# Turning tile rows with VectorE and SBUF-to-SBUF transfers in place of TensorE transposes

## Chip, cores and metric

One core of one Trainium2 chip. The metric is the device time of one execution in microseconds. The kernel before took 358.4 us (median of three runs, 358.2 to 358.91).

## What is computed

The input `x` has 64 batches of 32 rows with 256 features. Every batch goes through one attention layer and two MLPs, and then through three adapter layers whose weights are picked by the batch's role (one of three):

```python
attn = softmax((x @ Wq) @ (x @ Wk).T * scale)
attn_out = (attn @ (x @ Wv)) @ Wp + bp
cms_out = gelu(attn_out @ cW1 + cb1) @ cW2 + cb2 + one_hot(code)
x1 = clip(x + cms_out + gelu(concat(attn_out, cms_out) @ mW1 + mb1) @ mW2 + mb2, 0, 1)
for layer in range(3):            # x1 is the first hidden_states
    h = gelu(hidden @ W_down[role] + b_down[role]) @ W_up[role] + b_up[role]
    hidden = layernorm(hidden + h) * gamma[role] + beta[role]
```

## The kernel before

The 2048 rows are sorted by role and cut into 16 tiles of 128 rows, four batches each. A tile is "pure" if its four batches have one role. Tiles 4 and 5 (`MIXED`) take what is left over: their four batches have four sets of weights, so each of their layers loads four weight blocks of 256.5 KB where a pure tile loads one.

The MLPs run over groups of rows: three groups of 512 rows and two of 256 (`GROUPS`). Their steps are written in a list: "H n" computes the hidden block n on TensorE, "D n" brings it down into the results, and between them ScalarE makes the gelu and a high part (`h_hi`) and VectorE the low part (`h_lo`). TensorE is fed by one matmul after another this way.

The three adapter layers of the tiles lie between these steps. While group 1 runs, tiles 0 to 3 go through their layers (wave 1); while group 2 runs, tiles 4 to 7 (wave 2); then tiles 8 to 11 and 12 during the two small groups, and the last three at the end. A wave has 14 spots, one behind an H step each, and in a wave each tile starts one spot behind the one before. For a tile and layer, the down product is at one spot, the up product one spot on, the norm two spots on, and the next layer's down product four spots on. "(4, 1)" below is tile 4, layer 1, with layers counted from 0.

The down product needs the tile with features on the partitions, while the norm leaves rows there. So for layers 1 and 2 `half` on TensorE turns the normed rows `window_x` by two 128x128 transposes into a PSUM bank (L1512), and ScalarE copies it to `window_xT` (L841), which the down product reads (L1481; L1478 for mixed tiles). Layer 0 reads `xT`, which is there already.

SyncE's queue carries nearly all loads. It works through the items (tile, layer) in the order of their down products, weights of an item first (`window_weights`), then the rows (gamma, beta, and for layer 0 an up bias) of the item before (`window_rows`). Mixed tiles' layer 1 weights lie in a region that the attention uses until it is done (`at_done`). For each mixed tile at layer 0 it reads four roles from a table (L572) and then waits for `at_done`:

```python
roles_of[w] = ([role(MIXED[0] + WIN * MIXED.index(w) + q) for q in range(WIN)] if w in MIXED ...
if w in MIXED:
    if layer == 0:
        sp.wait_ge(at_done, VB * NG)
```

TensorE's down product of a mixed tile waits for all four of its blocks.

Of the kernel before, what the change touches and what calls it, by code (L numbers as in the profile page):

```python
# [12 lines left out]
P = 128  # L13
# [29 lines left out]

ROLE_COLS = NW - len(MIXED) + MIXED_BATCHES
# [12 lines left out]
def build(nc, x, codes, roles, Wq, Wk, Wv, Wp, bp, cW1, cb1, cW2, cb2, mW1, mb1, mW2, mb2, adapters, out):  # L57
# [3 lines left out]
    with ExitStack() as ctx:  # L61
# [107 lines left out]
        window_xT = sb("window_xT", [P, 2, VB, P])  # L169
        window_h = sb("window_h", [P, 2, P])  # L170

# [84 lines left out]
        earlier_ready = sem("earlier_ready")  # L256
        role_row_ready = sem("role_row_ready")
        roles_turned = sem("roles_turned")
        own_ready = sem("own_ready")
        roles_counted = sem("roles_counted")  # L260
# [6 lines left out]
        code_ready = sem("code_ready")  # L267
# [55 lines left out]
        emptied = {b: sem(f"emptied{b}") for b in (2, 3, 5, 6, 7)}  # L323
        first_w_in = sem("first_w_in")
# [89 lines left out]
        def turned(wave, spot):  # L414
            return [(w, at // 4 + 1) for w, at in turns(wave, spot) if at % 4 == 3 and 1 <= at // 4 + 1 < LAYERS]
# [94 lines left out]
        def _(sp):  # L510
# [76 lines left out]
            def window_weights(w, layer):  # L587
                slot, k = slot_of(w), item(w, layer)
                if layer == 0:
                    roles_of[w] = ([role(MIXED[0] + WIN * MIXED.index(w) + q) for q in range(WIN)] if w in MIXED  # L590
                                   else [role(role_col(w))])
# [12 lines left out]

# [307 lines left out]
        def _(dve):  # L912
# [3 lines left out]
            dve.tensor_scalar(earlier[:, :], batch_id[:, :], own_id[0:B, 0:1], None, ALU.is_gt).then_inc(earlier_ready, 1)  # L916
# [19 lines left out]
            dve.tensor_tensor(own_onehot[:, :], role_id[:, :], own, ALU.is_equal).then_inc(own_ready, 1)  # L936
# [4 lines left out]
            dve.wait_ge(own_ready, 1)  # L941
            dve.wait_ge(roles_counted, 1)
# [18 lines left out]
            dve.tensor_scalar(code_rep[:, :], ones[:, :], code_col[:, :], None, ALU.mult).then_inc(code_ready, 1)  # L961
# [31 lines left out]
            def attention_part(stage_name, g):  # L993
# [18 lines left out]
                if stage_name == "P":  # L1012
# [6 lines left out]
                    dve.wait_ge(pd_clear, 2)  # L1019
# [653 lines left out]
```

## Time and profile before

| | |
|---|---|
| median of three runs | 358.4 us |
| profiled execution, its own time | 357.08 us |
| its span | 355.2 us |
| PE (TensorE) busy | 344.4 us, 97% |
| DVE (VectorE) busy | 202.6 us, 57% |
| ACT (ScalarE) busy | 169.2 us, 48% |
| DMA moved | 46.14 MB, mean 130 GB/s |

The span runs from the first instruction to the end of the last. "Busy" is the union of an engine's instructions; a matmul's duration in the records is longer than the distance to the next one's start, since they are pipelined.

### The profile page before, as it was taken

How to read it: one execution, taken by the hardware profiler on the slowest of the kernel's cores; microseconds unless marked ns; L12 is line 12 of the kernel's file. 1: busy time of each engine (PE TensorE's matmuls, PEld its weight loads, DVE VectorE, ACT ScalarE, POOL GpSimd, SP SyncE). 2: the span in 40 equal slices, each digit the busy share in tenths (PEclk: the TensorE clock that was granted, in tenths of full speed). 3: DMA queues.
4: the chain of work that ended last, by engine and by line, in shares of the span. 5: the costliest groups of instructions: out<-in, count | busy, mean ns of one | idle time of the engine just before them, and what ended most of it. 6: DMA issues, size and time to landing. Idle time of an engine off the chain costs nothing.

```text
span 355.2 us, 6665 instructions
## 1 busy us (share of the span) xinstructions
PE 344.4 (97%) x2252; PEld 287.1 (81%) x2252; DVE 202.6 (57%) x488; ACT 169.2 (48%) x338; POOL 62.0 (17%) x94
## 2 busy tenths in 40 slices
PE   7799999999999999999999999999999999999994
PEld 6587678787878888888886777877899999999962
DVE  5066375433353875466545666554589777554584
ACT  3555685453642563463336454443455544543421
POOL 2700230000040110012311111003322024100231
PEclk9999998999999999999999999999999999999998
DMA  6674899284020141310075898412856533188001
GB/s 211 199 221 146 206 126 144 57 192 109 2 54 6 60 119 62 101 49 6 25 253 163 226 257 306 104 31 74 227 145 188 168 104 108 59 273 345 23 2 45
DMA packets 30646, 46.14 MB, mean 130 GB/s; under 512 B 4779, under 2 KB 15348, under 8 KB 30612
## 3 DMA queue, kind: packets, MB, share of 16 engines
q1 hardware_dynamic: 28852, 41.72, 43.0%
q0 software_dynamic: 1392, 3.80, 3.9%
q8 instruction: 18, 0.29, 0.4%
q10 hardware_dynamic: 368, 0.20, 0.2%
q14 instruction: 16, 0.13, 0.1%
HBM read 43.60 MB, written 4.48 MB: 135 GB/s over the span
## 4 chain that ended last, share of the span: by engine, by line
PE 91%; ACT 3%; DVE 2%; issue 2%; POOL 1%; POOLq 0%; DVEq 0%
PE bank L332 12%; PE bank L334 12%; PE bank L333 12%; PE bank L1437 9%; PE bank L1442 8%; PE bank L1438 8%; PE bank L1481 4%; PE bank L1460 4%; PE bank L1343 2%; PE bank L1361 2%; PE bank L1512 2%; PE bank L1301 2%; PE bank L1242 1%; PE bank L1560 1%; PE bank L1457 1%
## 5 line engine op out<-in xcount | busy, mean ns | idle before, releaser
L798 ACT ACTIVATE h_full<-bank,bias 128x512 f32<-128x512 f32 (+1 forms) x80 | 48.2, 603 | 108.3 <-PE bank L334 98.0
L1035 DVE TENSOR_TENSOR h_lo<-h_full,h_hi 128x512 fp32r<-128x512 f32 (+1 forms) x80 | 46.8, 585 | 63.2 <-ACT h_hi L802 60.8
L718 POOL TENSOR_TENSOR rstd<-moments,minus_half 128x1 f32<-128x1 f32 x39 | 24.3, 623 | 168.1 <-DVE moments L1101 167.9
L802 ACT ACTIVATE h_hi<-h_full 128x512 fp32r<-128x512 f32 (+1 forms) x80 | 43.7, 547 | 2.5
L1093 DVE TENSOR_TENSOR window_y<-bank,window_x 128x256 f32<-128x256 f32 x39 | 16.5, 423 | 38.3 <-PE bank L1460 28.9
L1437 PE MATMUL bank<-h_hi,c_hi 128*128 128x512 f32 (+1 forms) x80 | 30.8, 393 | 0.2
L1437 PE MATMUL bank<-h_hi,m_hi 128*128 128x512 f32 (+1 forms) x80 | 30.2, 387 | 0.2
L332 PE MATMUL bank<-at_hi,c_hi 128*128 128x512 f32 (+1 forms) x80 | 29.3, 366 | 0.0
L332 PE MATMUL bank<-at_hi,m_hi 128*128 128x512 f32 (+1 forms) x80 | 29.2, 364 | 0.0
L334 PE MATMUL bank<-at_lo,c_hi 128*128 128x512 f32 (+1 forms) x80 | 27.9, 348 | 0.0
L334 PE MATMUL bank<-at_lo,m_hi 128*128 128x512 f32 (+1 forms) x80 | 27.8, 348 | 0.0
L333 PE MATMUL bank<-at_hi,m_lo 128*128 128x512 f32 (+1 forms) x80 | 27.8, 347 | 0.0
L333 PE MATMUL bank<-at_hi,c_lo 128*128 128x512 f32 (+1 forms) x80 | 27.8, 347 | 0.0
L1438 PE MATMUL bank<-h_hi,c_lo 128*128 128x512 f32 (+1 forms) x80 | 27.6, 354 | 0.0
L690 POOL DMA_INDIRECT xr<-in_x,row_idx x16 | 16.4, 1025 | 62.5 <-PE bank L1343 52.9
L1438 PE MATMUL bank<-h_hi,m_lo 128*128 128x512 f32 (+1 forms) x80 | 27.2, 349 | 0.0
L332 PE MATMUL bank<-cms_hi,m_hi 128*128 128x512 f32 (+1 forms) x70 | 24.3, 346 | 0.0
L333 PE MATMUL bank<-cms_hi,m_lo 128*128 128x512 f32 (+1 forms) x70 | 24.3, 346 | 0.0
L334 PE MATMUL bank<-cms_lo,m_hi 128*128 128x512 f32 (+1 forms) x70 | 24.3, 346 | 0.0
L1442 PE MATMUL bank<-h_lo,c_hi 128*128 128x512 f32 (+1 forms) x80 | 22.4, 362 | 0.1
L1084 DVE SCALAR_TENSOR_TENSOR window_x<-window_y,rstd,adapter_rows 128x256 f32<-128x256 f32 x39 | 18.7, 480 | 4.9 <-POOL rstd L718 3.2
L1442 PE MATMUL bank<-h_lo,m_hi 128*128 128x512 f32 (+1 forms) x80 | 21.4, 348 | 0.0
(239 smaller groups left out, 733.9 us busy)
## 6 DMA issues: line engine op xcount, KB each, us to landing
adapter_w<-packed_w SPq DMA_DIRECT2D x44, 256.5 KB, 3.5
adapter_rows<-packed_rows SPq DMA_DIRECT2D x36, 256.0 KB, 5.2
stage<-in_L_cond_mW SPq DMA_DIRECT2D x6, 512.0 KB, 6.3
mixed_w<-packed_w SPq DMA_DIRECT2D x8, 256.5 KB, 5.0
stage<-in_L_cond_cW SPq DMA_DIRECT2D x4, 512.0 KB, 4.7
last_w<-packed_w SPq DMA_DIRECT2D x2, 769.5 KB, 6.4
up_bias<-in_L_cond_b_up SPq DMA_DIRECT2D x12, 128.0 KB, 6.1
adapter_rows<-packed_rows SPq DMA_DIRECT2D x24, 64.0 KB
```

The source lines that it names most:

```text
L332: pe.matmul(o, w_hi_ap, r_hi_ap, start=first, stop=False)
L333: pe.matmul(o, w_lo_ap, r_hi_ap, start=False, stop=False)
L334: return pe.matmul(o, w_hi_ap, r_lo_ap, start=False, stop=last)
L718: pool.tensor_tensor(slot.rstd[:, :], slot.moments[:, 1:2], minus_half[:, :], ALU.pow)\
L798: act.activation(h_full[:, n % 2, rows], bank[n % 2][:, rows], ACT.Gelu, bias=bias[:, b:b + 1])\
L802: act.activation(h_hi[:, n % 2, rows], h_full[:, n % 2, rows], ACT.Copy).then_inc(h_hi_ready, 1)
L1035: dve.tensor_tensor(h_lo[:, n % 2, rows], h_full[:, n % 2, rows], h_hi[:, n % 2, rows].bitcast(F32), ALU.subtract).then_inc(h_lo_ready, 1)
L1084: dve.scalar_tensor_tensor(slot.x[:, :], slot.y[:, :], slot.rstd[:, :], slot.rows[:, 1, :], ALU.mult, ALU.add).then_inc(slot.x_ready, 1)
L1093: dve.tensor_tensor(slot.y[:, :], bank[6][:, 0:V], slot.x[:, :], ALU.add).then_inc(emptied[6], 1)
L1437: pe.matmul(results[ob][:, rows], high(cols), h_hi[:, n % 2, rows], start=(j == 0), stop=False)
L1438: pe.matmul(results[ob][:, rows], low(cols), h_hi[:, n % 2, rows], start=False, stop=False)
L1442: ins = pe.matmul(results[ob][:, rows], high(cols), h_lo[:, n % 2, rows], start=False, stop=(j == HB - 1))
```

## The change

For tiles 0 to 7 (`SPREAD`), the 16 turns for layers 1 and 2 leave TensorE and ScalarE. VectorE turns `window_x` in 32x32 blocks into a new tile `block_rows`, and SyncE's queue then moves the blocks by four transfers, one for each quarter of 32 rows, into `window_xT`, of which there are now three instead of two. A transfer carries 128 pieces of 256 bytes. The down product waits for the transfers' semaphore. SyncE waits for VectorE before each move, and for the down product three moves back.

The loads of the mixed tiles change their place. After `at_done`, `mixed_weights_ahead` reads the roles and loads all four layer 1 blocks and two of the four layer 0 blocks, for tile 4 and then for tile 5. The other two blocks of layer 0 follow for each tile. The rows of item (3, 2) go ahead of the wait for `at_done` instead of behind the first mixed weights. Four semaphores of the setup are merged into others, with the same waits.

```diff
+SPREAD = WAVES[1] + WAVES[2]
+RING = 3
...
-        window_xT = sb("window_xT", [P, 2, VB, P])
+        window_xT = sb("window_xT", [P, RING, VB, P])
         window_h = sb("window_h", [P, 2, P])
+        block_rows = sb("block_rows", [P, 2, V])
...
-            return [(w, at // 4 + 1) for w, at in turns(wave, spot) if at % 4 == 3 and 1 <= at // 4 + 1 < LAYERS]
+            return [(w, at // 4 + 1) for w, at in turns(wave, spot)
+                    if at % 4 == 3 and 1 <= at // 4 + 1 < LAYERS and w not in SPREAD]
+
+        def spread(wave, spot):
+            return [(w, layer + 1) for w, layer in norms(wave, spot) if layer + 1 < LAYERS and w in SPREAD]
+
+        moves = {}
+        for wave in WAVES:
+            for spot in range(SPOTS):
+                for move in spread(wave, spot):
+                    moves[move] = len(moves)
+
+        def moved(n):
+            return next(move for move, m in moves.items() if m == n)
+
+        def blocks_of(n):
+            return window_xT[:, n % RING, :, :].rearrange("p k m -> p (k m)").rearrange("p (q k r) -> p q k r", q=Q, k=VB)
+
+        def move_is_in(engine, n):
+            engine.wait_ge(blocks_in[n % RING], 16 * Q * (n // RING + 1))
...
+                if layer == 0 and w not in MIXED:
+                    roles_of[w] = [role(role_col(w))]
                 if w in MIXED:
                     if layer == 0:
-                        sp.wait_ge(at_done, VB * NG)
                         sp.wait_ge(slot.x_ready, k)
                     elif layer == 2:
                         sp.wait_ge(filled[6], use["U", w, 0] + 1)
-                    for q in range(WIN):
+                    for q in ((0, 1), (), range(WIN))[layer]:
                         load_w(batch_w(w, layer, q), roles_of[w][q], layer, mixed_in[MIXED.index(w)][layer % 2])
                 else:
                     if k >= 2:
                         sp.wait_ge(slot.x_ready, k if w - SLOTS in MIXED and layer == 0 else k - 1)
                     load_w(slot.w[:, k % 2, :], roles_of[w][0], layer, slot.w_in[k % 2])
+
+            def mixed_weights_ahead():
+                sp.wait_ge(at_done, VB * NG)
+                for n, w in enumerate(MIXED):
+                    roles_of[w] = [role(MIXED[0] + WIN * n + q) for q in range(WIN)]
+                    for q in range(WIN):
+                        load_w(batch_w(w, 1, q), roles_of[w][q], 1, mixed_in[n][1])
+                    for q in range(2, WIN):
+                        load_w(batch_w(w, 0, q), roles_of[w][q], 0, mixed_in[n][0])
+
+            def move_blocks(w, layer):
+
+                n = moves[w, layer]
+                sp.wait_ge(blocks_turned, n + 1)
+                if n >= RING:
+                    sp.wait_ge(filled[7], use["D", *moved(n - RING)] + 1)
+                for q in range(Q):
+                    sp.dma_start(blocks_of(n)[:, q, :, :].rearrange("p k r -> p (k r)"),
+                                 block_rows[quarter(q), n % 2, :].rearrange("p (f m) -> p f m", f=Q))                        .then_inc(blocks_in[n % RING], 16)
...
             for n, w, layer in items:
+                if n and items[n - 1][1:] in moves:
+                    move_blocks(*items[n - 1][1:])
+                if (w, layer) == (MIXED[0], 0):
+                    window_rows(*items[n - 1][1:])
+                    mixed_weights_ahead()
                 window_weights(w, layer)
-                if 0 < n <= len(items) - len(ending):
+                if 0 < n <= len(items) - len(ending) and (w, layer) != (MIXED[0], 0):
                     window_rows(*items[n - 1][1:])
...
+                for w, layer in spread(wave, spot):
+                    n = moves[w, layer]
+                    dve.wait_ge(slot_of(w).x_ready, item(w, layer - 1) + 1)
+                    if n >= 2:
+                        move_is_in(dve, n - 2)
+                    dve.transpose(block_rows[:, n % 2, :].rearrange("p (f k r) -> p k f r", f=Q, k=VB),
+                                  slot_of(w).x[:, :].rearrange("p (k i f) -> p k f i", f=Q, k=VB)).then_inc(blocks_turned, 1)
...
+                    elif w in SPREAD:
+                        move_is_in(pe, moves[w, layer])
...
-                        rows = (xT[:, vb, columns(w)] if layer == 0
-                                else window_xT[:, order["T", w, layer] % 2, vb, :])
+                        rows = (xT[:, vb, columns(w)].rearrange("p (q r) -> p q r", q=Q) if layer == 0
+                                else blocks_of(moves[w, layer])[:, :, vb, :] if w in SPREAD
+                                else window_xT[:, order["T", w, layer] % 2, vb, :].rearrange("p (q r) -> p q r", q=Q))
```

On TensorE, at the first removed pair (`xT` is the layer 0 start of tile 1; `window_x0` is tile 0's rows). Before:

```order
L1442 MATMUL bank2<-h_lo,c_hi 128x512 [waits h_lo_ready]
L1442 MATMUL bank3<-h_lo,c_hi 128x512
L1504 MATMUL bank6<-ident,xT 128x128 [waits emptied6]
L1504 MATMUL bank6<-ident,xT 128x128
L1512 MATMUL bank7<-ident,window_x0 128x128 [waits emptied7,window_x_ready0]
L1512 MATMUL bank7<-ident,window_x0 128x128
L332 MATMUL bank0<-at_hi,c_hi 128x512 [waits gelu_done]
L333 MATMUL bank0<-at_hi,c_lo 128x512
```

The same place on TensorE now:

```order
L1491 MATMUL bank2<-h_lo,c_hi 128x512 [waits h_lo_ready]
L1491 MATMUL bank3<-h_lo,c_hi 128x512
L1556 MATMUL bank6<-ident,xT 128x128 [waits emptied6]
L1556 MATMUL bank6<-ident,xT 128x128
L333 MATMUL bank0<-at_hi,c_hi 128x512 [waits gelu_done]
L334 MATMUL bank0<-at_hi,c_lo 128x512
```

The two transposes of `window_x0` are gone; nothing took their place.

On VectorE, where tile 0's rows come out of the norm (`window_x0`), before:

```order
L1084 SCALAR_TENSOR_TENSOR window_x0<-window_y0,rstd0,adapter_rows0 128x256 [waits norm_step0,rstd_ready0]
L1093 TENSOR_TENSOR window_y1<-bank6,window_x1 128x256 [waits emptied6,filled6]
L1035 TENSOR_TENSOR h_lo<-h_full,h_hi 128x512 [waits h_hi_ready]
L1099 BN_STATS stats1<-window_y1 128x6 [waits emptied6]
L1101 BN_AGGR moments1<-stats1 128x2 [waits norm_step1]
```

The same place on VectorE now:

```order
L1126 SCALAR_TENSOR_TENSOR window_x0<-window_y0,rstd0,adapter_rows0 128x256 [waits norm_step0,rstd_ready0]
L1135 TENSOR_TENSOR window_y1<-bank6,window_x1 128x256 [waits emptied6,filled6]
L1141 STREAM_TRANSPOSE block_rows<-window_x0 128x2x4x32 [waits window_x_ready0]
L1077 TENSOR_TENSOR h_lo<-h_full,h_hi 128x512 [waits h_hi_ready]
L1148 BN_STATS stats1<-window_y1 128x6 [waits emptied6]
L1150 BN_AGGR moments1<-stats1 128x2 [waits norm_step1]
```

The block transpose stands ahead of the next `h_lo`. From the third move on it also waits for the move two back (`blocks_in`).

On SyncE's queue, where it waits for the attention's end (`adapter_w0` and `mixed_w4` are the four layer 0 blocks of tile 4; the roles were read ahead of this wait), before:

```order
L575 ISA [waits window_x_ready0,at_done]
L575 DMA adapter_w0<-packed_w 128x513
L575 ISA
L575 DMA adapter_w0<-packed_w 128x513
L575 ISA
L575 DMA mixed_w4<-packed_w 128x513
L575 ISA
L575 DMA mixed_w4<-packed_w 128x513
L579 ISA [waits window_x_ready3]
L579 DMA adapter_rows3<-packed_rows 128x512
L572 TENSOR_LOAD role_table
```

The same wait on SyncE's queue now (`second_w` is a layer 1 block):

```order
L592 TENSOR_LOAD role_table [waits at_done]
L592 ISA x2
L592 TENSOR_LOAD role_table
L592 ISA x2
L592 TENSOR_LOAD role_table
L592 ISA x2
L592 TENSOR_LOAD role_table
L592 ISA x2
L595 ISA
L595 DMA second_w<-packed_w 128x513
L595 ISA
L595 DMA second_w<-packed_w 128x513
```

Behind it stand two more layer 1 blocks of tile 4, two of its layer 0 blocks, four role reads and six blocks for tile 5. Only then, on the same queue, comes the rest of layer 0:

```order
L595 DMA mixed_w5<-packed_w 128x513
L595 ISA
L595 DMA mixed_w5<-packed_w 128x513
L595 ISA [waits window_x_ready0]
L595 DMA adapter_w0<-packed_w 128x513
L595 ISA
L595 DMA adapter_w0<-packed_w 128x513
L595 ISA [waits window_x_ready1]
L595 DMA adapter_w1<-packed_w 128x513
L595 ISA
L595 DMA adapter_w1<-packed_w 128x513
```

The last block of (4, 0) was the fourth load behind the wait, with its roles read already; it is now the fourteenth, with eight role reads between.

## Rows read from the trace of the kernel before

**Rows 1.** The page: span, and busy time by engine.

```profile
span 355.2 us, 6665 instructions
...
PE 344.4 (97%) x2252; PEld 287.1 (81%) x2252; DVE 202.6 (57%) x488; ACT 169.2 (48%) x338; POOL 62.0 (17%) x94
```

**Rows 2.** The page: the chain that ended last, by engine.

```profile
PE 91%; ACT 3%; DVE 2%; issue 2%; POOL 1%; POOLq 0%; DVEq 0%
```

**Rows 3.** Line L1512, 110 to 255 us: duration min/median/max, first and last start.

```profile
L1512 PE MATMUL bank<-ident,window_x x32: 270/272/273, 126.7 to 246.0; 128*128 128x128 f32 x32
```

**Rows 4.** Timeline of PE (start, us): with a pair, and without.

```profile
130.12 0.63 PE L1442 MATMUL bank<-h_lo,c_hi 128*128 128x512 f32 x2
130.58 0.38 PE L1512 MATMUL bank<-ident,window_x 128*128 128x128 f32 x2
...
131.03 0.39 PE L333 MATMUL bank<-at_hi,c_lo 128*128 128x512 f32 x1
...
138.41 0.62 PE L1442 MATMUL bank<-h_lo,c_hi 128*128 128x512 f32 x2
...
139.10 0.39 PE L333 MATMUL bank<-at_hi,m_lo 128*128 128x512 f32 x1
```

**Rows 5.** Timeline of PE at the first D step of the second MLP: with, without.

```profile
145.01 0.39 PE L334 MATMUL bank<-cms_lo,m_hi 128*128 128x512 f32 x1
...
145.81 0.40 PE L1438 MATMUL bank<-h_hi,m_lo 128*128 128x512 f32 x1
...
68.44 0.39 PE L334 MATMUL bank<-cms_lo,m_hi 128*128 128x512 f32 x1
...
69.25 0.40 PE L1438 MATMUL bank<-h_hi,m_lo 128*128 128x512 f32 x1
```

**Rows 6.** Groups of VectorE by form: busy us, mean ns, idle before.

```profile
L1035 DVE TENSOR_TENSOR h_lo<-h_full,h_hi 128x512 fp32r<-128x512 f32 x48 | 33.2, 692 | 51.6 <-ACT h_hi L802 50.2 <-issue 1.3
...
L1093 DVE TENSOR_TENSOR window_y<-bank,window_x 128x256 f32<-128x256 f32 x39 | 16.5, 423 | 38.3 <-PE bank L1460 28.9 <-PE bank L1457 8.1 <-issue 1.3
...
L1021 DVE STREAM_TRANSPOSE pd<-expd 32x128 f32<-32x128 f32 x16 | 4.8, 303 | 0.3
```

**Rows 7.** Timeline: norm and next down product, tiles 0 and 4, layer 0 to 1.

```profile
120.28 0.47 DVE L1084 SCALAR_TENSOR_TENSOR window_x<-window_y,rstd,adapter_rows 128x256 f32<-128x256 f32 x1
...
128.75 0.61 PE L1481 MATMUL bank<-window_xT,adapter_w 128*128 128x128 f32 x4
...
198.16 0.48 DVE L1084 SCALAR_TENSOR_TENSOR window_x<-window_y,rstd,adapter_rows 128x256 f32<-128x256 f32 x1
...
207.44 0.65 PE L1478 MATMUL bank<-second_w,window_xT 128*32 128x128 f32 x16
```

**Rows 8.** SyncE's longest wait, 155 to 195 us, and its timeline behind it.

```profile
SPq L575 <- PE bank L334: 11.2, 1, 11.2
...
177.53 0.87 SPq L575 DMA_DIRECT2D adapter_w<-packed_w  x2
...
179.64 0.33 SPq L579 DMA_DIRECT2D adapter_rows<-packed_rows  x1
182.50 0.86 SPq L575 DMA_DIRECT2D adapter_w<-packed_w  x2
```

**Rows 9.** Weight loads 177 to 186 us, and small stores: issue to landing.

```profile
DMA to landing us min/median/max: 2.7/3.4/4.5
...
out<-last_x SPq DMA_DIRECT2D x4, 32.0 KB, 1.6
```

**Rows 10.** Stretch 179 to 183 us: busy by engine, PEclk, DMA share, GB/s.

```profile
179.00:183.00 4.00, 4.00 (x19) 3.29 (x18) 0.54 (x2) 1.47 (x3) 0.65 (x1) 1.00 0.92 329
```

**Rows 11.** Timeline of PE: the down product of (4, 0) starts.

```profile
190.52 0.30 PE L1478 MATMUL bank<-adapter_w,xT 128*32 128x128 f32 x2
```

**Rows 12.** The one stretch at the low clock, and the matmuls ahead of it.

```profile
59.80:63.20 3.40, 3.40 (x10) 2.62 (x9) 0.25 (x3) 0.00 (x0) 0.00 (x0) 0.50 0.63 73
...
L1373 PE MATMUL bank<-acol,prep_w x24: 165/250/250, 56.2 to 58.6; 128*128 128x1 f32 x24
```

More of the change, by code:

```diff
@@ L255, in build @@
         id_consts = sem("id_consts")
-        earlier_ready = sem("earlier_ready")
         role_row_ready = sem("role_row_ready")
         roles_turned = sem("roles_turned")
-        own_ready = sem("own_ready")
-        roles_counted = sem("roles_counted")
         more_consts = sem("more_consts")
@@ L266, in build @@
         onehot_ready = sem("onehot_ready")
-        code_ready = sem("code_ready")
         rows_turned = sem("rows_turned")
@@ L323, in build @@
         emptied = {b: sem(f"emptied{b}") for b in (2, 3, 5, 6, 7)}
+        blocks_turned = sem("blocks_turned")
+        blocks_in = [sem(f"blocks_in{n}") for n in range(RING)]
         first_w_in = sem("first_w_in")
@@ L588, in window_weights @@
                 slot, k = slot_of(w), item(w, layer)
-                if layer == 0:
-                    roles_of[w] = ([role(MIXED[0] + WIN * MIXED.index(w) + q) for q in range(WIN)] if w in MIXED
-                                   else [role(role_col(w))])
+                if layer == 0 and w not in MIXED:
+                    roles_of[w] = [role(role_col(w))]
                 if w in MIXED:
                     if layer == 0:
-                        sp.wait_ge(at_done, VB * NG)
                         sp.wait_ge(slot.x_ready, k)
@@ L915, in _ @@
             dve.wait_ge(id_consts, 3)
-            dve.tensor_scalar(earlier[:, :], batch_id[:, :], own_id[0:B, 0:1], None, ALU.is_gt).then_inc(earlier_ready, 1)
+            dve.tensor_scalar(earlier[:, :], batch_id[:, :], own_id[0:B, 0:1], None, ALU.is_gt).then_inc(pd_clear, 1)
             for a in (first_attention, second_attention):
@@ L935, in _ @@
             own = own_role.to_broadcast([B, ROLES])
-            dve.tensor_tensor(own_onehot[:, :], role_id[:, :], own, ALU.is_equal).then_inc(own_ready, 1)
+            dve.tensor_tensor(own_onehot[:, :], role_id[:, :], own, ALU.is_equal).then_inc(role_row_ready, 1)
             dve.tensor_tensor(upto, role_id[:, :], own, ALU.is_le)
@@ L940, in _ @@
             link(dve.tensor_copy(own_role_col[:, :], own_role))
-            dve.wait_ge(own_ready, 1)
-            dve.wait_ge(roles_counted, 1)
+            dve.wait_ge(role_row_ready, 2)
+            dve.wait_ge(roles_turned, 2)
             link(dve.tensor_copy(counts_i[:, :], totals))
@@ L960, in _ @@
             dve.wait_ge(more_consts, 2)
-            dve.tensor_scalar(code_rep[:, :], ones[:, :], code_col[:, :], None, ALU.mult).then_inc(code_ready, 1)
+            dve.tensor_scalar(code_rep[:, :], ones[:, :], code_col[:, :], None, ALU.mult).then_inc(onehot_ready, 1)
             dve.wait_ge(rows_turned, 1)
@@ L1018, in attention_part @@
                                            a.row_sum[:, 1, :].unsqueeze(2).to_broadcast([P, GT, T]), ALU.mult))
-                    dve.wait_ge(pd_clear, 2)
+                    dve.wait_ge(pd_clear, 3)
                     for q in range(Q):
@@ L1255, in _ @@
             pe.matmul(bank[4][0:B, 0:1], role_row[:, 1, :], ones[0:1, 0:1], start=True, stop=True).then_inc(roles_turned, 1)
-            pe.wait_ge(earlier_ready, 1)
-            pe.wait_ge(own_ready, 1)
+            pe.wait_ge(pd_clear, 1)
+            pe.wait_ge(role_row_ready, 2)
             pe.matmul(bank[5][0:B, 0:ROLES], ones[:, 0:B], own_onehot[:, :], start=True, stop=True)
             pe.matmul(bank[5][0:B, ROLES:2 * ROLES], earlier[:, :], own_onehot[:, :], start=True, stop=True)\
-                .then_inc(roles_counted, 1)
+                .then_inc(roles_turned, 1)
             turn_weights(0)
@@ L1271, in _ @@
             fold_weights(0, wT[:, 0], wT[:, 1])
-            pe.wait_ge(code_ready, 1)
+            pe.wait_ge(onehot_ready, 2)
             pe.matmul(bank[6][:, 0:B], code_rep[:, :], onehot[:, :], start=True, stop=True)
@@ L1477, in after @@
                             for q in range(WIN):
-                                ins = pe.matmul(bank[b][quarter(q), 0:KD], rows[:, quarter(q)], batch_w(w, layer, q)[:, down],
+                                ins = pe.matmul(bank[b][quarter(q), 0:KD], rows[:, q, :], batch_w(w, layer, q)[:, down],
                                                 start=(vb == 0), stop=(vb == VB - 1))
```

## Prediction, made before the changed kernel ran

> **What bounds the kernel now.** I read the page's busy times first: TensorE is busy for 344.4 of 355.2 us, and no other engine passes 57% [rows 1]. The chain of work that ended last lies on TensorE for 91% [rows 2]. Since a matmul's recorded end is modelled, a busy share doesn't prove that nothing waits, so I then read the timeline of PE for the distances from start to start. Between 110 and 255 us, where the two waves of the change lie, a 512-column matmul follows the last one every 0.23 us (0.69 for three [rows 4]), and the few longer steps are changes of form. So in this stretch TensorE's own instruction stream is the time. What leaves it is gained one to one, and what makes TensorE wait is lost one to one, since I see no later idle time that could give it back.
>
> The second thing to read is the load queue. SyncE sat 11.2 us in its longest wait of the stretch, until the attention's last product (bank, L334), and issued the first mixed weights right behind it, at 177.53 [rows 8]. TensorE wants them at 190.52 [rows 11]. This distance of 13 us is what the moved loads must fit into.
>
> **The change part by part.**
>
> *The transposes go.* 32 of them run between 126.7 and 246.0 us [rows 3], that is 16 pairs. Their recorded 272 ns is not what they cost. With a pair, the start of the two L1442 matmuls and that of L333 lie 131.03 - 130.12 = 0.91 us apart; at a like place without one, 139.10 - 138.41 = 0.69 [rows 4]. A pair costs 0.22 us. Two of the 16 cost nothing: where the second MLP's first D step waits for its `h_hi`, L334 to L1438 takes 145.81 - 145.01 = 0.80 with the pair and 69.25 - 68.44 = 0.81 without [rows 5]. The pair only filled a wait there, and this holds for tiles 3 and 7 at layer 1. So 14 x 0.22 = 3.1 us are gained. The Trainium skill, on the page "TensorE: Matmul & The Clock Gate", section "Part 4: PE-mode transpose", gives about 275 ns for one transpose in a kernel's context. The trace's 272 ns agrees as a duration; taken as a cost it would make the gain 32 x 0.275 = 8.8 us. The distances in the timeline decide for 3.1.
>
> *ScalarE loses 16 copies.* It is no bound, and nobody waits for it in this stretch but for `h_hi` at the two places above. Worth nothing; never a loss.
>
> *VectorE gets 16 block transposes.* The trace has none of 128x256. A block transpose of half the width takes 303 ns, an addition of the full width 423 ns [rows 6]. I take 0.42 us and allow 0.3 to 0.8. It stands ahead of the next `h_lo`, and the 48 large `h_lo` had 51.6 us of idle time before them, over 1 us each in the mean [rows 6]. Where there is less, TensorE still reads an `h_lo` only one D and one H step on, twelve matmuls of 0.23 us or more. So it costs nothing; without that cover, it would be 16 x 0.4 = 6.4 us.
>
> *The moves.* SyncE issues four transfers of 32 KB, one every 0.53 us (two span 0.87 and one 0.33 [rows 8]): 2.1 us. Nearest to their landing are the 32 KB stores at the end, 1.6 us, and the weight loads under traffic, 2.7 to 4.5 us [rows 9]. From the end of the norm to the data this is 0.4 (another addition on VectorE) + 0.4 + 2.1 + 1.6 to 4.5 = 4.5 to 7.4 us. The shortest distance of the 16 is that of (0, 1): 128.75 - 120.75 = 8.0 us [rows 7]; next is (4, 1) with 207.44 - 198.64 = 8.8 [rows 7], and the others reach to 18. So they are hidden. Queued behind SyncE's wait for a move are the weights and rows of the next items, whose products come later still.
>
> *The mixed loads.* Here I count every instruction of the queue. Before, TensorE's product (4, 0) needed the first four loads behind the wait. The last of them was issued at 179.1 (0.53 ahead of the rows' 179.64 [rows 8]) and landed at 183.6 (4.5, the maximum of [rows 9]), 7 us early. Now the order is: four role reads, six loads, four role reads, six loads, then the two that complete (4, 0). From the end of one issue to the next with four role reads between takes 182.50 - 179.97 = 2.5 us instead of 0.2 [rows 8], so the reads add 2.3. The first load is issued at 177.5 + 2.3 = 179.8, the sixth at 179.8 + 5 x 0.53 = 182.5, the seventh at 182.5 + 0.3 + 2.5 = 185.3, and the fourteenth at 185.3 + 7 x 0.53 = 189.0. Unhindered it lands at 189.0 + 2.7 = 191.7, after the 190.5 at which TensorE stands before it. But eight loads issued at 0.53 us run into each other: at the measured 329 GB/s [rows 10] one of 262.7 KB takes 0.80 us. The first of the eight lands at 185.3 + 2.7 = 188.0, the last at 188.0 + 7 x 0.80 = 193.6. In the burst of before, the fourth load landed at 183.6, which is 0.9 later than this reckoning gives (180.2 + 3 x 0.80 = 182.6); at that burst's own pace, (183.6 - 180.2) / 3 = 1.12, the last of eight would land at 195.8. I take 193.6 + 0.9 = 194.5, since the straggling is nearly the same for every load and doesn't grow with their number. TensorE waits 194.5 - 190.5 = 4.0 us, at least 1.2, at most 5.3. The first wave's gain doesn't change this, since it shifts `at_done` and (4, 0) alike. Before, this cost was hidden by 7 us of slack; the layer 1 blocks, needed only at 207.4 [rows 7], now take it up.
>
> What is late next: the rows of (4, 0) are eight issues behind all sixteen loads, so they go out until 189.0 + 2 x 0.53 + 8 x 0.5 = 194, some 5 us later than before, and those of (5, 0) follow. VectorE would wait for them, but TensorE is itself 4 us late by then, and the remaining microsecond is less than the distance by which `h_lo` is early. I put it at nothing. Behind it the queue has eight loads less to issue, and the moves of wave 2 start on an almost empty queue.
>
> *The sum.* -3.1 + 4.0 = +0.9. Against the profiled execution's own 357.08 (span 355.2 and 1.9 around it) this is 358.0. The median of the runs shown lies 1.3 higher, 358.4, so I forecast 359.3.
>
> **Rivals.** A measurement of this kernel tells about 0.2%, 0.7 us.
>
> *A. As above, the wait at (4, 0) eats the gain.* +0.9, from -0.6 to +1.7: 42%. About half of this is within 0.7.
>
> *B. The weights come faster.* If loads run into each other less than they did in the burst, and land near the issue bound, the wait is 1.2 to 2.3 and the result -1.9 to -0.8, 357.0: 20%. For it speaks that shorter parts of the burst moved well over 329 GB/s; against it, that every load of that burst landed later than its issue bound.
>
> *C. No wait at all,* the gain stands whole: -3.1, 355.3: 5%. It needs the fourteenth load to land before 190.5, when it is hardly issued.
>
> *D. The wait also drops TensorE's clock.* The granted clock was at the lower level, 1.2 GHz, once in this trace after the start, for 3.4 us from 59.8, right after 24 matmuls of one column [rows 12], that is with hardly any work in the array; otherwise it was 2.4. A wait of 4 us is as little work. If the clock falls for such a stretch, half of 3.4 us is lost, 1.7: +2.6, 361.0: 15%. The Trainium skill, page "TensorE: Matmul & The Clock Gate", section "Part 1: The HAM clock gate (the "warmup" mystery)", says that the clock returns to 1.2 GHz when the engine has been idle. The trace shows a fall after thin work, and no run so far one after a wait.
>
> *E. The moves come late in wave 2.* Pieces of 256 bytes queue behind the mixed layer 2 blocks or each other, VectorE waits for the move two back with `h_lo` behind it, and TensorE waits for that. The moves must take more than the 8.8 us that (4, 1) has. One second-wave move late by 4 us, what a load under full traffic takes, gives +4.9 with A, 363; late by 1 us, +1.9. For it: the queue is dense there. Against: it has eight loads less. 12%, and 6% for what I don't see.
>
> **How the numbers follow.** Faster by over 0.2% are C, B but for a tail, and a rim of A: 25%. Within it lies half of A and that tail: 25%. Slower are the rest of A, D, E: 50%. The range takes in the bounds of A, nearly all of B, and D: 356.6 to 361.3. What is left out is C, and the long end of E.
>
> **What would show it.** In the profile of the changed kernel TensorE should have 32 matmuls less and, at the down product of (4, 0), an idle stretch of about 4 us that ends with a DMA of `adapter_w` or `mixed_w`. SyncE's first load behind `at_done` should come 2.3 us after the wait ends. The 14 places of the pairs should be 0.22 us shorter, and the two others as long as before. The block transpose should take 0.3 to 0.8 us, no down product should wait for `window_xT`'s transfers, and DMA should run near 330 GB/s for the 14 us behind `at_done`. I am wrong if that idle stretch is under 2 us, or if another of a microsecond stands in wave 2, or if the clock isn't at its upper level behind the wait.

## The result, and the profile after

The changed kernel takes 362.88 us (median of 7 runs, 361.49 to 366.21). The kernel before, run beside it, takes 358.2 us (357.08 to 358.91, 7 runs). The ratio is 1.0147, 95% interval 1.0112 to 1.0183: slower by about 5 us. Disturbed runs are left out of this and all later ratios, but not of the medians (the run of `loads_only` that was profiled is one). Forecast were 359.3 us and a range up to 361.3. The side was right; the size was outside the range.

The profiled execution of the changed kernel is its slowest, 366.21 us. The page, with span and busy time by engine, then the chain that ended last (compare [rows 1, 2]):

```profile
span 364.3 us, 6658 instructions
...
PE 347.3 (95%) x2220; PEld 288.0 (79%) x2220; DVE 210.3 (58%) x504; ACT 164.2 (45%) x322; POOL 61.6 (17%) x94
...
PE 78%; DVE 6%; issue 4%; ACT 4%; SPq 3%; DMA 3%; POOL 2%; POOLq 0%; DVEq 0%
```

TensorE has 32 matmuls less and is busy 2.9 us longer, in a span 9.1 us longer. The chain, which lay on TensorE for 91%, lies there for 78% and now runs over VectorE, SyncE's queue and DMA too. The timeline of PE shows where it leaves TensorE:

```profile
193.28 0.40 PE L335 MATMUL bank<-at_lo,c_hi 128*128 128x512 f32 x1
198.77 0.43 PE L1530 MATMUL bank<-adapter_w,xT 128*32 128x128 f32 x2 [5.09 <-DMA adapter_w<-packed_w]
```

This is the down product of tile (4, 0), at the place where the kernel before had none of it [rows 11]: TensorE stands still for 5.09 us and is released by the second of the tile's last two layer 0 blocks.

Stretches by time, with the busy us of PE, PEld, DVE, ACT and POOL, then PEclk, DMA share and GB/s. The first three lie around the wait; the last two are early in the run:

```profile
190.14:193.50 3.36, 3.27 (x14) 2.17 (x12) 2.55 (x6) 1.74 (x3) 1.03 (x1) 1.00 0.88 257
193.68:198.77 5.09, 0.00 (x0) 0.00 (x0) 0.69 (x1) 1.32 (x2) 0.00 (x0) 0.86 0.98 357
197.32:204.15 6.83, 5.38 (x28) 4.09 (x29) 0.42 (x1) 1.10 (x5) 0.00 (x0) 0.50 0.72 217
...
16.42:19.83 3.41, 3.10 (x10) 2.12 (x8) 0.00 (x0) 0.96 (x3) 1.83 (x2) 0.50 0.81 264
60.79:67.62 6.83, 6.83 (x19) 5.52 (x19) 1.93 (x5) 0.29 (x1) 0.00 (x0) 0.50 0.46 67
```

The third row is new: the granted clock is 0.50 of 2.4 GHz, that is 1.2 GHz, from 197.32, after 3.6 us without a matmul, to 204.15. TensorE works in it for the 5.38 us from 198.77. If all of that work took twice its time, half of it, 2.7 us, is lost; this is an estimate, and `busy_wait` below measures 2.4. The last two rows are most of why this one execution is the slowest. The changed code starts only behind 110 us, and such early stretches come and go from run to run: the profile of before has one of 3.4 us at 59.80 [rows 12], the traces below have none or one, and that of `loads_only` has the same two. The low clock behind the wait isn't of this kind. The mean granted clock is 0.986 or less in all seven runs of the changed kernel, and 0.991 or more in the seven of the kernel before that ran beside the first four experiments.

To compare traces without this noise I count from the first transpose of `xT` (tile 1's start, in front of all that the change touches) to the end of the span. Instructions that read `ident` between 100 and 250 us, with duration min/median/max and first and last start; first the kernel before:

```profile
L1504 PE MATMUL bank<-ident,xT x16: 270/272/273, 113.7 to 205.2; 128*128 128x128 f32 x16
```

and the changed kernel:

```profile
L1556 PE MATMUL bank<-ident,xT x16: 270/272/421, 117.7 to 215.9; 128*128 128x128 f32 x16
```

Before, this stretch is 355.2 - 113.7 = 241.5 us; after, 364.3 - 117.7 = 246.6. The difference of +5.1 agrees with the difference of the medians, 4.7.

Its parts are -3.1 for the pairs, +5.1 for the wait, +2.7 for the clock, and two small waits. One is this, on PE and VectorE around the start of tile (1, 0), where the kernel before had none:

```profile
124.72 0.41 DVE L1135 TENSOR_TENSOR window_y<-bank,window_x 128x256 f32<-128x256 f32 x1
...
125.05 0.62 DVE L1141 STREAM_TRANSPOSE block_rows<-window_x 128x256 f32<-128x256 f32 x1
...
125.61 0.64 DVE L1077 TENSOR_TENSOR h_lo<-h_full,h_hi 128x512 fp32r<-128x512 f32 x1
...
127.28 0.41 DVE L1161 TENSOR_TENSOR window_x<-bank,up_bias 128x256 f32<-128x256 f32 x1
...
127.84 0.67 PE L1509 MATMUL bank<-adapter_w,window_h 128*128 128x256 f32 x2 [0.50 <-DVE window_x L1161]
```

VectorE works without a pause here, the block transpose in the middle of it, and is late with `window_x`, so that TensorE waits 0.50 us. The other is 0.15 us at 165.62, behind the attention's `pd`. In sum -3.1 + 5.1 + 2.7 + 0.65 = +5.35, against the measured +5.1; with 2.4 for the clock it is +5.05.

The new instructions, over the whole run (duration min/median/max, and for the moves the time from issue to landing):

```profile
L639 SPq DMA_DIRECT2D window_xT<-block_rows x64: 549/597/1542, 125.7 to 250.8; - x64
L1141 DVE STREAM_TRANSPOSE block_rows<-window_x x16: 622/633/681, 125.0 to 248.3; 128x256 f32<-128x256 f32 x16
...
DMA to landing us min/median/max: 1.9/1.9/2.6
```

A block transpose takes 0.63 us, the issue of one transfer 0.60, its landing 1.9. SyncE's queue around the wait (start, and the time over which a group of issues extends):

```profile
183.26 2.20 SPq L595 DMA_DIRECT2D second_w<-packed_w  x4
185.65 0.86 SPq L595 DMA_DIRECT2D mixed_w<-packed_w  x2
188.94 1.41 SPq L595 DMA_DIRECT2D second_w_rest<-packed_w  x3
190.55 0.33 SPq L595 DMA_DIRECT2D second_w<-packed_w  x1
191.07 1.99 SPq L595 DMA_DIRECT2D mixed_w<-packed_w  x2
193.24 2.05 SPq L595 DMA_DIRECT2D adapter_w<-packed_w  x4
195.48 0.51 SPq L599 DMA_DIRECT2D adapter_rows<-packed_rows  x1
```

Six loads, a hole for four role reads, six, and the four that complete layer 0. The first four role reads stand ahead of the first line, from 180.5 on. The names tell the regions of the layer 1 blocks (`second_w`, `second_w_rest`) and of layer 0 (`adapter_w`, `mixed_w`). The fourteenth load, which (4, 0) waits for, is the second of the last four. It went out at 193.75, and TensorE started at 198.77, 5.0 us later.

### The profile page after: what moved, and what is told of

Same layout as the page of the kernel before. It is cut to its first block, busy times and chain, and to the rows that moved or that the text cites. A ratio compares the mean times of both kernels' runs of the same rounds, so it can differ in the third digit from the quotient of the medians.

```text
span 364.3 us, 6658 instructions
## 1 busy us (share of the span) xinstructions
PE 347.3 (95%) x2220; PEld 288.0 (79%) x2220; DVE 210.3 (58%) x504; ACT 164.2 (45%) x322; POOL 61.6 (17%) x94
## 4 chain that ended last, share of the span: by engine, by line
PE 78%; DVE 6%; issue 4%; ACT 4%; SPq 3%; DMA 3%; POOL 2%; POOLq 0%; DVEq 0%
PE bank L333 10%; PE bank L334 10%; PE bank L335 10%; PE bank L1486 8%; PE bank L1491 7%; PE bank L1487 7%; PE bank L1533 3%; PE bank L1509 3%; PE bank L1350 2%; PE bank L1392 2%; PE bank L1410 2%; SPq L595 2%; ACT h_full L840 1%; DMA adapter_w<-packed_w 1%; ACT h_hi L844 1%
## 5 line engine op out<-in xcount | busy, mean ns | idle before, releaser
L1486 PE MATMUL bank<-h_hi,c_hi 128*128 128x512 f32 (+1 forms) x80 | 31.8, 406 | 0.2
L1486 PE MATMUL bank<-h_hi,m_hi 128*128 128x512 f32 (+1 forms) x80 | 30.2, 387 | 0.3
L1487 PE MATMUL bank<-h_hi,c_lo 128*128 128x512 f32 (+1 forms) x80 | 28.6, 366 | 0.0
L335 PE MATMUL bank<-at_lo,c_hi 128*128 128x512 f32 (+1 forms) x80 | 27.9, 349 | 0.0
L335 PE MATMUL bank<-at_lo,m_hi 128*128 128x512 f32 (+1 forms) x80 | 27.8, 347 | 0.0
L335 PE MATMUL bank<-cms_lo,m_hi 128*128 128x512 f32 (+1 forms) x70 | 24.3, 346 | 0.0
```

The lines of the kernel that those rows point to most:

```text
L335: return pe.matmul(o, w_hi_ap, r_lo_ap, start=False, stop=last)
L1486: pe.matmul(results[ob][:, rows], high(cols), h_hi[:, n % 2, rows], start=(j == 0), stop=False)
L1487: pe.matmul(results[ob][:, rows], low(cols), h_hi[:, n % 2, rows], start=False, stop=False)
```

## Experiments

The expectations speak of the kernel before at 358.1 or 358.2 us. `turns_only`, `loads_only`, `busy_wait` and `roles_first` ran on one chip, with the kernel before at a median of 358.02 us (7 runs); the other four ran on another, with the kernel before at 358.25 (21 runs). Between the two sets, ratios compare better than medians.

**1. The new turns with the old order of loads** (`turns_only`). `mixed_weights_ahead` is gone, and `window_weights` and the loop are those of before:

```diff
-                    for q in ((0, 1), (), range(WIN))[layer]:
+                    for q in range(WIN):
...
-                if (w, layer) == (MIXED[0], 0):
-                    window_rows(*items[n - 1][1:])
-                    mixed_weights_ahead()
```

> The changed kernel with the mixed loads back in the order of before (roles read ahead of the wait, four layer 0 blocks behind it, layer 1 blocks later). My theory: the turns are worth 3.1 us and the whole loss lies in the new load order, so 355.1 against 358.2, with no wait at the product of (4, 0). Rival 1: the moves themselves cost (late behind other loads in wave 2, or VectorE waits for them): 357 to 359, with idle time of TensorE at a down product that reads moved blocks. Rival 2: the old order was left because the moves of (4, 1) and (5, 1) queue behind the eight layer 1 blocks: a wait of 1 to 4 us at those two.

Measured: 356.75 us (356.25 to 356.89), ratio 0.9969 (0.9945 to 0.9993). Faster, but by 1.27 us and not by the 3.1 that I expected. The waits of its PE timeline, besides those of 0.49 and 0.14 us that the changed kernel has too:

```profile
188.70 0.74 PE L1481 MATMUL bank<-h_lo,c_hi 128*128 128x512 f32 x2 [0.43 <-issue]
...
212.72 0.31 PE L1520 MATMUL bank<-second_w_rest,window_xT 128*32 128x128 f32 x3 [0.80 <-issue]
```

and on VectorE, ahead of the first of them:

```profile
184.53 0.49 DVE L1143 SCALAR_TENSOR_TENSOR window_y<-window_y,moments,adapter_rows 128x256 f32<-128x256 f32 x1 [0.80 <-DMA adapter_rows<-packed_rows]
...
187.96 0.68 DVE L1067 TENSOR_TENSOR h_lo<-h_full,h_hi 128x512 fp32r<-128x512 f32 x1
```

With the old order the rows of (3, 2) come behind the first mixed weights and hold VectorE up; from there it works without a pause, and the `h_lo` that the product at 188.70 reads is done at 188.64. The layer 1 product of tile 5 then waits 0.80 us, and the trace tells for what. The last of its four weight blocks was issued at 205.57 and landed 4.8 us later, at 210.4, before the wait began. VectorE's turn for it began at 204.05, but its four transfers, behind these weights and the rows on SyncE's queue, went out from 208.80 to 210.69, and the last signal of their semaphore came at 212.63. So the move is what was late, as rival 2 had it, by less than its 1 to 4 us. The waits sum to 0.49 + 0.14 + 0.43 + 0.80 = 1.9, and 3.1 - 1.9 = 1.2 is near the 1.27 us by which the median fell; the stretch from the first `xT` transpose to the end is only 0.7 shorter than before (355.1 - 114.2 = 240.9 us). So the turns by themselves are a gain, and small waits take more than half of it. None of the later versions has the first of the last two waits, since the change moved the rows; I had counted neither.

**2. The new order of loads alone** (`loads_only`), with the turns on TensorE. The diff is that part of the change:

```diff
+            def mixed_weights_ahead():
+                sp.wait_ge(at_done, VB * NG)
...
+                if (w, layer) == (MIXED[0], 0):
+                    window_rows(*items[n - 1][1:])
+                    mixed_weights_ahead()
```

> The kernel before with nothing but the new order of the mixed loads. My theory: TensorE waits some 5 us at the product of (4, 0) as in the changed kernel, and its clock falls to 1.2 GHz behind it for some 2.5 us more, so 358.2 + 5 + 2.5 = 365.7. Rival: the loads are late only because the moves share their queue; then the wait is under 2 us and the time 358 to 360.

Measured: 363.72 us (362.92 to 368.57), ratio 1.0159 (1.0126 to 1.0192). Its PE timeline and the stretch of low clock behind:

```profile
199.77 0.43 PE L1488 MATMUL bank<-adapter_w,xT 128*32 128x128 f32 x2 [4.70 <-DMA adapter_w<-packed_w]
...
197.79:204.62 6.83, 4.85 (x27) 3.66 (x28) 0.18 (x1) 0.94 (x5) 0.00 (x0) 0.50 0.82 239
```

The whole loss is here without a single move: a wait of 4.70 us, and by the same estimate 4.85 / 2 = 2.4 us for the clock. The rival is out. The time is 2 us under the 365.7 that I expected: the medians rose by 5.7 us and not by 7.5, while the stretch from the first `xT` transpose to the end grew by 366.7 - 118.2 - 241.5 = 7.0. For the moves' pieces of 256 bytes, should they crowd out the weights, the 0.4 us between 4.70 and 5.09 is left; no run tests this by itself.

**3. TensorE kept busy during the wait** (`busy_wait`). Twenty-two 512-column matmuls, whose result nobody reads, go ahead of the product of (4, 0):

```diff
+                    if (w, layer) == (MIXED[0], 0):
+                        pe.wait_ge(emptied[b], use["D", w, layer])
+                        for _ in range(FILL):
+                            pe.matmul(bank[b][:, :], high(slice(0, P)), at_hi[:, 0, 0, :], start=True, stop=True)
```

> The changed kernel with 22 extra matmuls of 512 columns (22 x 0.23 = 5.1 us, results unused) on TensorE just ahead of its wait at (4, 0). My theory: the wait ends at the same moment, the matmuls fit into it, the clock stays at its upper level, and what the clock cost comes back: 362.9 - 2.5 = 360.4. Rival 1: the fall of the clock has nothing to do with the wait: 362.9. Rival 2: the work comes on top: 367 or more.

Measured: 359.73 us (359.17 to 360.12), ratio 1.0054 (1.0028 to 1.008), 3.15 us below the changed kernel. On PE:

```profile
188.94 5.15 PE L1518 MATMUL bank<-at_hi,c_hi 128*128 128x512 f32 x22
194.23 0.30 PE L1535 MATMUL bank<-adapter_w,xT 128*32 128x128 f32 x2
```

TensorE does 5 us of useless work, then waits 0.15. The product comes 194.23 - 188.71 = 5.5 us behind the last matmul before the wait (198.77 - 193.28 = 5.5 in the changed kernel). The wait is as long, but the clock stays at 2.4 GHz, and the stretch from the first `xT` transpose to the end is 357.4 - 113.2 = 244.2 us, 2.4 less than after. From the product of (4, 0) to the end it is 357.4 - 194.2 = 163.2 us against 364.3 - 198.8 = 165.5. So the clock costs 2.3 or 2.4 us by the traces and 3.15 by the medians; half of 5.38 us, 2.7, lies between.

**4. Half of it kept busy** (`half_busy`), `FILL = 11`.

> The changed kernel with 11 matmuls of 512 columns, whose result nobody reads, ahead of the product of tile (4,0) (22 of them kept the clock up): TensorE works for about 2.5 us of the wait of 5.1 us and stands idle for the rest, about 2.5 us. The loads are the same, so the wait's own end is the same, and only the clock's reaction can change the time. If a wait of about 2.5 us still brings the fall of the clock to 1.2 GHz for 6.83 us: about 362.9 us. If it doesn't: about 359.7 us, as with 22.

Measured: 361.67 us (359.68 to 362.83, 8 runs), ratio 1.0086 (1.005 to 1.0121). Neither figure, but between them. By the medians it is 1.9 us above `busy_wait` and 1.2 below the changed kernel, by the ratios 1.1 above and 2.2 below, and its interval overlaps both; the trace has to decide. On PE, and the clock behind the wait:

```profile
195.37 0.30 PE L1535 MATMUL bank<-adapter_w,xT 128*32 128x128 f32 x2 [2.82 <-DMA adapter_w<-packed_w]
...
196.27:199.68 3.41, 3.41 (x11) 2.70 (x10) 0.32 (x1) 0.89 (x5) 0.00 (x0) 0.50 0.73 180
```

A wait of 2.82 us also brings the fall, but for 3.41 us in place of 6.83, all of it under work: 1.7 us by the same estimate. From the product of (4, 0) to the end it is 360.3 - 195.4 = 164.9 us, 1.7 more than in `busy_wait`. I had expected either all of the clock's cost or nothing. It comes in steps.

**5. Roles read ahead of the wait for `at_done`** (`roles_first`):

```diff
             def mixed_weights_ahead():
-                sp.wait_ge(at_done, VB * NG)
                 for n, w in enumerate(MIXED):
                     roles_of[w] = [role(MIXED[0] + WIN * n + q) for q in range(WIN)]
+                sp.wait_ge(at_done, VB * NG)
+                for n, w in enumerate(MIXED):
```

> The changed kernel with all eight role reads ahead of the wait for the attention's end, the loads in its own order. If the reads between the loads make the wait (2.3 us each time), the loads start 2.3 us earlier and run without a pause: at 0.80 us per load the fourteenth lands about 191.5 on the scale of before, the wait at (4, 0) is about 1 us and the clock stays up: 358.2 - 3.1 + 1 = 356.1. Rival: the pace of the loads alone makes it; at the 1.12 us per load of the old burst the wait is still 4.3 us, and with the clock 361 to 362.

Measured: 356.42 us (354.31 to 359.08), ratio 0.9966 (0.9916 to 1.0017). On PE:

```profile
191.32 0.30 PE L1531 MATMUL bank<-adapter_w,xT 128*32 128x128 f32 x2 [1.16 <-DMA adapter_w<-packed_w]
```

Eight reads of the role table in the wrong place are 3.9 us of the 5.1, and all of the clock: behind a wait of 1.16 us it stays up in this trace. The expected 356.1 and wait of 1 us came. The interval of this run alone still touches 1. The stretch from the first `xT` transpose to the end is 354.4 - 114.3 = 240.1 us, 6.5 below after and 1.4 below before.

**6. Layer 0 blocks first** (`layer0_first`). As 5, and all eight blocks of layer 0 go ahead of the eight of layer 1:

```diff
-                    for q in ((0, 1), (), range(WIN))[layer]:
+                    for q in ((), (), range(WIN))[layer]:
...
                 for n, w in enumerate(MIXED):
+                    sp.wait_ge(slot_of(w).x_ready, item(w, 0))
                     for q in range(WIN):
-                        load_w(batch_w(w, 1, q), roles_of[w][q], 1, mixed_in[n][1])
-                    for q in range(2, WIN):
                         load_w(batch_w(w, 0, q), roles_of[w][q], 0, mixed_in[n][0])
+                for n, w in enumerate(MIXED):
+                    for q in range(WIN):
+                        load_w(batch_w(w, 1, q), roles_of[w][q], 1, mixed_in[n][1])
```

> The changed kernel with the eight role reads ahead of the wait for at_done, then the layer 0 blocks of all eight roles, then the layer 1 blocks of all eight (the rows of tile (3,2) stay ahead). My theory: at the product of tile (4,0) every layer 0 block is needed, so with eight blocks ahead of it in place of fourteen, at some 1.0 us a block, the 1.16 us that it still waited with the roles alone goes. What stays are the 0.5 us at the pair of (1,0), where VectorE is late, and some 0.15 us in wave 2: 3.1 - 0.65 = 2.45 us below the kernel before, about 355.6 us against 358.1, and the clock stays up. The rival: the rows of tile (4,0) or the moves of wave 2 are late behind sixteen loads in a row, or the layer 1 product of (5,1) waits; then 356 to 358 us with a wait shown there.

Measured: 354.56 us (353.51 to 356.38, 6 runs), ratio 0.991 (0.9875 to 0.9945). This is the fastest version, 1 us below what I expected. TensorE doesn't wait at (4, 0). The 0.50 at (1, 0) and the 0.14 stay, and there is a new one, shown on PE with the time to landing of the move's four transfers (issued from 198.38 on):

```profile
205.82 0.65 PE L1533 MATMUL bank<-second_w,window_xT 128*32 128x128 f32 x16 [0.59 <-issue]
...
DMA to landing us min/median/max: 3.8/4.6/4.8
```

This is the product of (4, 1). Its last transfer landed at 205.73. A transfer took 4.6 us here in place of 1.9. The rows of tiles 4 to 7 stand ahead of it in the queue; that these hold it up is argued, not shown. They aren't the whole cause. In `roles_first` the same rows stand ahead, and the product of (4, 1) doesn't wait. In both traces the first transfer goes out 9.9 us behind the product of (4, 0) (201.23 - 191.32, 198.38 - 188.46). But the four issues took 2.5 us there and 3.3 here, since the second alone took 1.37 in place of 0.60. This 0.8 us is more than the wait. The stretch to the end is 352.5 - 112.6 = 239.9 us, 1.6 below before, where -3.1 + 0.50 + 0.14 + 0.59 = -1.9 was due. The medians say -3.7. Its profiled run has no early low-clock stretch, where that of before had one at 59.80 [rows 12]; such noise may be part of the 3.7. The interval reaches from 0.9875 to 0.9945.

**7. The block transposes later on VectorE** (`late_turn`). As 6, with the loop over `spread` moved from behind the addition into `window_y` to behind the last step of `after` (which makes the `window_x` that TensorE waited for):

```diff
-                for w, layer in spread(wave, spot):
...
                     dve.tensor_tensor(slot.x[:, :], bank[b][:, 0:V], slot.up_bias[:, :], ALU.add).then_inc(emptied[b], 1)
+                for w, layer in spread(wave, spot):
```

> As layer0_first, with VectorE's block transposes of a tile put behind the last step of VectorE's part of the tile rather than ahead of it. My theory: the 0.5 us wait at the pair of (1,0) comes from the 0.63 us block transposes that stand ahead of the sum TensorE waits for; behind it they delay nothing that TensorE needs, and the wait goes: 355.6 - 0.5 = 355.1 us. The rival: the moves that hang on the block transposes are now too late for the product of (0,1), and TensorE waits there instead, by up to 0.5 us or more: the same as layer0_first or slower.

Measured: 357.84 us (355.46 to 360.08, 12 runs), ratio 0.9998 (0.9968 to 1.0027), 3.3 us above `layer0_first`. The expected 355.1 us didn't come. The wait at (1, 0) is gone, so its cause was the block transpose. But on PE:

```profile
160.81 0.38 PE L1395 MATMUL bank<-pd,xr 128*128 128x128 f32 x1 [1.17 <-DVE pd L1066]
...
207.38 0.65 PE L1533 MATMUL bank<-second_w,window_xT 128*32 128x128 f32 x16 [1.81 <-issue]
```

The attention's `pd` comes behind the turn now and costs 1.17 us, and the move of (4, 1) is 1.81 us late (its first transfer went out at 202.37 against 198.38, the last landed at 207.29). Behind that wait the clock fell once more in this run:

```profile
208.29:211.70 3.41, 3.41 (x10) 2.61 (x9) 0.99 (x3) 0.88 (x5) 0.15 (x1) 0.50 0.30 77
```

Not in every run: four of the twelve have a mean granted clock of 0.997 or more, and a stretch of 3.41 us at half the clock would alone bring it to 0.995. In sum -3.1 + 1.17 + 1.81 + 1.7 = +1.6, against 355.4 - 112.5 = 242.9 us, +1.4. The rival's mechanism is what came, at (4, 1) and not at (0, 1), where I had put it.

**8. The removed work done twice** (`pairs_twice`), in the kernel before:

```diff
-                    for vb in range(VB):
+                    for vb in list(range(VB)) * (2 if w < 8 else 1):
```

> The kernel before, with every turned pair of the tiles 0 to 7 (two transposes) issued twice, so that the removed work is done twice over; the output is the same. My theory: a pair costs 0.22 us of TensorE's time where TensorE is the bound, not the 0.53 to 0.55 us that the records of its two transposes show: 16 x 0.22 = +3.5 us, about 361.6 us against 358.1. The rival: the recorded durations count, 16 x 0.54 = +8.6 us, about 366.7 us.

Measured: 361.44 us (360.48 to 362.64), ratio 1.0109 (1.0069 to 1.0149), +3.2 us. The timeline of PE at the place of [rows 4]:

```profile
130.43 0.63 PE L1442 MATMUL bank<-h_lo,c_hi 128*128 128x512 f32 x2
130.90 0.60 PE L1512 MATMUL bank<-ident,window_x 128*128 128x128 f32 x4
...
131.57 0.39 PE L333 MATMUL bank<-at_hi,c_lo 128*128 128x512 f32 x1
```

The distance is 131.57 - 130.43 = 1.14 us with two pairs, 0.91 with one and 0.69 with none [rows 4]. A pair costs 0.23 us. The expected 3.5 us came, and the 8.6 of the recorded durations are out.

## Why the forecast was wrong

**The pairs: right.** 0.22 us each stands in the distances of three kernels and in the time of `pairs_twice`. The two pairs that were to save nothing saved nothing: from L335 to L1486 it is 0.47 us in the changed kernel at 148.85 and 0.46 at 232.02, as at 72.45, where there never was a pair. The recorded durations would have given over two and a half times as much.

**The wait at (4, 0): the right place and cause, too small.** Forecast 4.0 us, measured 5.09, within the bound of 5.3. (With that bound the sum reaches -3.1 + 5.3 = +2.2, and not the +1.7 at which rival A ended.) The first load came 183.26 - 180.5 = 2.8 us after the wait for `at_done` ended, a little more than the 2.3 that the reads were to add. Up to the seventh load the reckoning nearly holds: 188.94 - 183.26 = 5.7 us behind the first, forecast 5.5. Then came "the fourteenth at 185.3 + 7 x 0.53": the seven distances took 193.75 - 188.94 = 4.8 us, not 3.7. Nearly all of the excess is one issue, the second `mixed_w` of the line at 191.07, which took 1.47 us in place of 0.33; that full DMA engines (82% busy over these 4.8 us) held it up is argued, not shown. The landing was then 5.0 us after the issue, forecast 5.5. Over the 14 us from 183.26 the DMA moved 278 GB/s and not near 330. `loads_only`, `roles_first` and `layer0_first` show the cause in steps, with waits of 4.70, 1.16 and none.

**The clock: the failed step.** The sum has no term for it. It stood as rival D at 15% and 1.7 us, and the range took it in only beside a wait of 4.0; beside D's 1.7, the wait's own bound of 5.3 would have given 362.3. What the runs show is that the clock's fall belongs to the wait. In the traces it came behind the waits of 5.09, 4.70, 2.82 and 1.81 us, and not behind that of 1.16. In the changed kernel it lasted 6.83 us and not 3.4, and it cost 2.4 us by the trace of `busy_wait`, 2.7 by the estimate. `busy_wait` shows that it is idleness and not the late product that brings it. This alone moves 359.3 to 361.7 or 362, out of the range; without it the longer wait (+1.1) and the small waits (+0.65) would have given 361.05, still inside. The prediction's last sign of being wrong, a clock that isn't at its upper level behind the wait, is the one that came. The Trainium skill, page "TensorE: Matmul & The Clock Gate", section "Part 1: The HAM clock gate (the "warmup" mystery)", has this return to 1.2 GHz after idleness. The stretches at 0.50 behind the waits of 5.09 and 4.70 us agree with it. The prediction gave this little weight, since no run had shown a fall after a wait. But the trace of before shows one after idleness, at its very end, where TensorE's last matmul ends at 350.51:

```profile
350.51:353.34 2.83, 0.00 (x0) 0.00 (x0) 1.64 (x5) 0.00 (x0) 0.55 (x1) 1.00 0.24 65
353.34:355.20 1.86, 0.00 (x0) 0.00 (x0) 0.00 (x0) 0.00 (x0) 0.00 (x0) 0.50 0.27 71
```

After 2.8 us without a matmul the granted clock is 0.50. With this row, D belonged in the sum as soon as a wait of 4 us stood there.

**"So it costs nothing", of the block transposes: wrong by half a microsecond.** They take 0.63 us, inside 0.3 to 0.8 but half as much again as the 0.42 that I took. (The 32x128 transposes that I went by have half the width and a quarter of the partitions.) I argued from the mean idle time ahead of `h_lo` alone. The wait came elsewhere, behind `h_lo`, at the `window_x` of tile 1's start, in the one place where VectorE has no pause. `late_turn` shows the cause.

**The moves, rival E: nothing in the changed kernel.** No product waits for one there. Their issue is slower than I took (0.60 and not 0.53), the landing 1.9 us. E's mechanism is real all the same: without the long wait at (4, 0) a move is late by 0.80 us in `turns_only`, 0.59 in `layer0_first` and 1.81 in `late_turn`, though not in `roles_first`. In `layer0_first` block transpose to landing took 205.73 - 197.72 = 8.0 us, longer than the 0.4 + 2.1 + 4.5 = 7.0 of the upper bound. One term in front was too small as well: 0.4 us for the addition between the norm and the block transpose. In `roles_first` the norm of (4, 0) ends at 199.43 and the block transpose starts at 200.56, 1.1 us later, since that addition first waits 0.80 us for its bank.

**Rivals B and C** are refuted: loads did not come faster. **What is late next** was right for the changed kernel, where TensorE has no wait over 0.13 us in the two waves behind (4, 0). VectorE does wait for these rows, 2.93 us in `roles_first` and 3.00 in `layer0_first`, and TensorE not for VectorE.

What stays open: why single issues and transfers take so much longer at times (1.47 us for an issue, 4.6 for a transfer), and why the early low-clock stretches come and go.

## What to carry to other kernels

When work leaves the bounding engine, the gain is the distance between the starts of its neighbours, with and without it, and not its recorded duration. When a load is moved ahead, count every instruction that its queue now runs between the release and the load needed first, register reads too, and put the load needed first at the front: here one order of the sixteen loads and eight reads cost a wait of 5.1 us and another none. And a wait of some microseconds that you forecast for TensorE is priced with the low clock behind it, here half as much again. Look for the price in the trace that you have: the end of a kernel, where TensorE is already done, is a wait too.

## What the hardware showed that I had not expected

- The low clock came in two lengths: 3.41 us behind waits of 1.81 and 2.82 us, 6.83 us behind 4.70 and 5.09. Behind the two shorter waits it began only 0.9 us after the work had resumed (208.29 against 207.38, 196.27 against 195.37).
- A turn of 128x256 in 32x32 blocks takes 0.63 us on VectorE, against 0.42 for an addition of the same width.
- An SBUF-to-SBUF transfer of 32 KB in pieces of 256 bytes lands 1.9 us after its issue in the changed kernel (median), and took 4.6 us (median of four) in `layer0_first`, where the DMA engines were 70% busy from 198.38 to 205.73. The busy share alone doesn't tell which: at 66%, from 211 to 214 in the changed kernel, it is 2.3 us.
- Four reads of a register from the role table hold SyncE's queue for 2.4 us (186.51 to 188.94), longer than the issue of four loads does.
